# Attention's y in memory: from group by row by token, to token tile by row by group

## What is computed

```python
y = y + jnp.einsum('bhqk,bhkd->bhqd', ascores, av)
y = y.transpose(0, 2, 1, 3).reshape(B, T, C)
attn_out = jnp.einsum('btc,oc->bto', y, w_proj)
x = x + ga * attn_out
h = layernorm(x) * (1 + cb) + sb
logits = einsum('bsh,he->bse', h, gate_w)      # top 2 of 8, softmax of the two
x = x + gb * ffn(h)                            # ffn: the two chosen experts, weighted
```

## Time and profile before

| | us |
|---|---|
| median of 3 runs | 2641.78 (2641.4 to 2646.95) |
| the profiled execution's own time | 2640.58 |
| its span, first to last instruction | 2638.8 |
| attention, by the trace | about 780 to 1920 |
| projection of tiles 2 to 15 | 1928.9 to 2148 |
| expert loop | 2193 to 2626 |

### The profile page before, as it was taken

The page is one execution under the profiler, slowest core; times in us unless marked ns, Lnnn a source line. Parts: engine busy times, 40 slices in busy tenths (PEclk is TensorE's granted clock), DMA queues, the critical chain, the costliest instruction groups (busy, mean ns, idle before and its releaser), DMA issues. The chain is left out here.

```text
span 2638.8 us, 39402 instructions
## 1 busy us (share of the span) xinstructions
PE 2439.7 (92%) x13343; PEld 1605.5 (61%) x13343; DVE 1595.9 (60%) x3212; ACT 1061.0 (40%) x1896; POOL 1210.8 (46%) x825
## 2 busy tenths in 40 slices
PE   6789999899789999999999999998978978999997
PEld 4676777787654444444444444444467766888885
DVE  5544555501077777777777777777146564677765
ACT  3420111111155555555556565555512113444443
POOL 3451423300057767676767676667601122333332
PEclk9999999999889999999999999999989988999998
DMA  7346555421385233333324241513277846879875
GB/s 274 112 132 209 170 165 163 122 85 40 75 258 118 60 94 85 85 94 85 93 73 105 59 112 50 110 44 102 60 236 185 188 98 249 299 279 324 306 273 180
DMA packets 229523, 386.15 MB, mean 146 GB/s; under 512 B 44212, under 2 KB 100980, under 8 KB 229236
## 3 DMA queue, kind: packets, MB, share of 16 engines
q1 hardware_dynamic: 201652, 308.18, 41.1%
q0 software_dynamic: 17152, 50.38, 5.5%
q10 hardware_dynamic: 10560, 25.54, 3.3%
HBM read 285.00 MB, written 106.38 MB: 148 GB/s over the span
## 5 line engine op out<-in xcount | busy, mean ns | idle before, releaser
L1462 POOL TENSOR_TENSOR t_two<-t_prob 128x1024 f32<-128x1024 f32 (+1 forms) x320 | 688.4, 2171 | 172.6 <-ACT t_prob L1310 109.3
L1310 ACT ACTIVATE t_prob<-t_scores_psum 128x512 f32<-128x512 f32 (+3 forms) x1280 | 610.5, 537 | 376.3 <-PE t_scores_psum L1115 188.1
L1342 DVE TENSOR_REDUCE t_part<-t_seen_psum 128x1 f32<-128x512 f32 x768 | 480.8, 682 | 148.2 <-PE t_seen_psum L1093 143.6
L1093 PE MATMUL t_seen_psum<-t_k_stack,t_q_stack 96*128 96x512 f32 (+3 forms) x1283 | 512.7, 405 | 31.7 <-DVE t_part L1342 15.3
L1115 PE MATMUL t_scores_psum<-t_q_stack,t_k_stack 97*128 97x512 f32 (+3 forms) x1280 | 504.1, 405 | 6.3 <-ACT t_prob L1310 5.0
L1115 PEld LDWEIGHTS t_scores_psum<-t_q_stack,t_k_stack 97*128 97x128 f32 x1280 | 243.2, 191 | 304.1 <-ACT t_prob L1310 168.4
L1348 DVE CUSTOM_DVE_ANT_0 t_seen_psum<-t_seen_psum,t_causal 128x128 f32<-128x128 f32 (+3 forms) x515 | 250.5, 504 | 101.9 <-PE t_seen_psum L1093 90.9
L1137 PE MATMUL t_y_acc_psum<-t_prob,t_v 128*32 128x512 f32 (+3 forms) x2560 | 301.9, 544 | 0.0
L1093 PEld LDWEIGHTS t_seen_psum<-t_k_stack,t_q_stack 96*128 96x128 f32 x1283 | 252.2, 197 | 67.2 <-DVE t_part L1342 29.9
L1762 PE MATMUL acc_psum<-z_e_hi,z_x_hi 128*128 128x512 f32 x576 | 228.3, 396 | 0.0
L1764 PE MATMUL acc_psum<-z_e_hi,z_x_lo 128*128 128x512 f32 x576 | 225.4, 391 | 0.0
(11 more groups left out here) (247 smaller groups left out, 3733.1 us busy)
## 6 DMA issues: line engine op xcount, KB each, us to landing
z_raw<-in_expert_w SPq DMA_DIRECT2D x80, 512.0 KB, 6.2
z_spare<-in_expert_w SPq DMA_DIRECT2D x72, 512.0 KB, 6.9
f_w_raw<-in_wmod SPq DMA_DIRECT2D x8, 2048.0 KB, 9.8
t_q_stack<-scratch_q_hi SPq DMA_DIRECT2D x64, 256.0 KB, 5.0
t_k_stack<-scratch_k_hi SPq DMA_DIRECT2D x64, 256.0 KB, 5.3
f_w_raw<-in_w_attn SPq DMA_DIRECT2D x24, 512.0 KB, 6.6
t_both<-scratch_inverse SPq DMA_DIRECT2D x132, 64.0 KB, 2.1
t_y<-scratch_a_y SPq DMA_DIRECT2D x33, 256.0 KB
```

What stands on the lines that cost most here:

```text
L1093: nc.tensor.matmul(seen[:, n % BANKS, 0:width], q_stack[par][0:STACK, h, t0:t0 + P], k_stack[par][0:STACK, h, c * CH:c * CH + width], star ...
L1310: nc.scalar.activation(prob[:, step % RING, h, c0:CH], scores[:, score_bank(step, h), c0:CH], ACT.Exp, scale=1.0 / math.sqrt(D)).then_inc( ...
L1342: nc.vector.tensor_reduce(dst, seen[:, n % BANKS], AX.X, ALU.max).then_inc(seen_free, 1)
L1462: nc.gpsimd.tensor_tensor(two[:, pair % 2, heads, c0:CH], a, b, ALU.add).then_inc(two_ready, 1)
```

## The change

The two tensors of y lie in memory as [NT, P, G, P]: token tile, row of the group (partition), group, token of the tile. A store of one unit then writes, for each of the 4 token tiles of its quarter, 128 tokens of each partition: pieces of 512 bytes, 512 pieces instead of 128. A load of one token tile reads 4 KB in one piece for each partition, 128 pieces instead of 1024. The amounts are the same, and so are the instructions of all engines and their order; in SP's stream only the shapes of the 66 stores and 32 loads of y differ (128x512 becomes 128x4x128, 128x8x128 becomes 128x1024).

```diff
@@ attention: store(i, wi)
-                    sp.dma_start(dst[group_of(i, wi), :, qc * CH:(qc + 1) * CH].rearrange("g p n -> (g p) n"),
-                                 src).then_inc(stored, 16)
+                    sp.dma_start(dst[qc * TPC:(qc + 1) * TPC, :, group_of(i, wi), :].rearrange("t p g n -> p t (g n)"),
+                                 src.rearrange("p (t n) -> p t n", n=P)).then_inc(stored, 16)
@@ attention: loads of the first two token tiles
-                                sp.dma_start(dst.bitcast(F32), src[:, :, n * P:(n + 1) * P].rearrange("g p n -> p g n")).then_inc(tokens_loaded[n], 16)
+                                sp.dma_start(dst.bitcast(F32), src[n]).then_inc(tokens_loaded[n], 16)
@@ tail: load_y(n)
-                    sp.dma_start(dst[:, n % 2].bitcast(F32), src[:, :, n * P:(n + 1) * P].rearrange("g p n -> p g n")).then_inc(y_loaded[n % 2], 16)
+                    sp.dma_start(dst[:, n % 2].bitcast(F32), src[n]).then_inc(y_loaded[n % 2], 16)
@@ adaln_block
-    y_hi, y_lo = scratch("y_hi", [G, P, T]), scratch("y_lo", [G, P, T])
+    y_hi, y_lo = scratch("y_hi", [NT, P, G, P]), scratch("y_lo", [NT, P, G, P])
```

## The result

The change makes the kernel slower. Its median is 2653.78 us (20 runs, 2640.48 to 2668.82) against 2645.02 for the kernel before (20 runs, 2633.91 to 2662.73): ratio 1.0035, interval 1.0021 to 1.0049, about 9 us. The forecast of 2628 was wrong in size and sign. The profiled execution took 2656.89 us.

The account below looks back on a forecast made before the run. PE, busy 92% of the span, bounds the kernel, so only its waits and low clock can be won. Gains of 3.2 + 4.3 + 4.6 + 0.8 = 12.9 us from 2640.58 give 2627.7, forecast 2628, range 2618 to 2641.

Parts of the forecast that it names:

- Stores ... I cost them at nothing: Attention: stores of y go from 2 KB to 512-byte pieces, costed at nothing, with SP's 8.2 us to spare.
- Term A: Start of the tail: cheaper y loads let DVE's constants land sooner, gain 3.2 us, bounds 1.6 to 5.2.
- Terms B and C: Tail beside scatters: y lands sooner; tiles 8 and 9 gain 4.3 us, tiles 12 and 13 gain 4.6.
- the factor on y's time: Tail loads beside a scatter: 4 KB packets take 0.78 (510 ns) of eight small ones' 656; between 0.50 and 0.88.
- the scatter sets the pace: Tail beside a scatter: piece size does not matter, only 3.2 us at the tail's start is gained, 2637.4; chance 0.20.
- a packet sticks: Tail: 4 KB load packets stick beside a scatter, deciding from about 740 ns; kernel slower, 2650 us; chance 0.12.
- The clock term: Tail, tiles 9 and 13: shortened waits lose less clock, gain 0.8 us for both, between 0 and 3.
- the stores are dear after all: Stores of y: 512-byte pieces take 5 us instead of 2, mattering only together with something unseen; chance 0.02.

Follow-up runs that it names:

- old_small_stores: Kernel before, old order of y, each run of 128 tokens padded to 160, so stores and loads are in 512-byte pieces: 2650.05 us, 1.0040.
- late scatters: Kernel before and changed kernel, each with all scatters held back until the projection's tiles are turned: 2654.82 us (1.0050) and 2666.47 us (1.0096).
- before_early: Kernel before (also called early), with SP issuing the store of y ahead of the broadcasts of the next unit's inverse: 2626.61 us, 0.9950.
- best: Kernel before, with the store ahead of the inverse's broadcasts and the reload between the inverse's store and those broadcasts: 2622.06 us, 0.9932.
- paced: Kernel before, with the scatters of the first three batches spread, one pair behind each turned tile: 2643.64 us, 1.0019.
- after_best: Changed kernel, with the store ahead of the inverse's broadcasts and the reload between the inverse's store and those broadcasts: 2624.39 us, 0.9946.
- new_padded: Changed kernel with a ninth, unused group, so that rows of y lie 4.5 KB apart instead of 4 KB: 2645.19 us, 1.0015.
- after_early: Changed kernel, with SP issuing the store of y ahead of the broadcasts of the next unit's inverse: 2628.63 us, 0.9947.
- old_large_loads: Kernel before, old layout and 2 KB stores, y loaded in 4 KB pieces in wrong order, comparable only up to the experts: 2706.44 us, 1.0223.
- new_small_loads: Changed kernel, same layout and small stores, loads of y cut into 512-byte pieces by taking even and odd groups apart: 2657.72 us, 1.0066.

## Why the prediction was wrong

**The step that failed first: "Stores ... I cost them at nothing".** Its cover was "nobody in attention waits for them but the reload of the adapter's part steps later", with SP's 8.2 us to spare. That slack is the end of the stage. The reload itself had none: DVE already waited 12.7 us for it in 15 places, and the row was there to be read. I named the waiter and did not ask whether it was late. In its place the runs showed that the small stores cost about 9 us: old_small_stores pays 1.0040 with nothing changed but the pieces and their padding. And three edits that take this chain off the path (no reload, store first, reload first as well) bring the medians of the two layouts to -5.6, +2.0 and +2.3 us of each other, where they are 8.8 and, with late scatters, 11.7 us apart. One such pair alone says little. With 95% intervals that I estimate from the single runs, the means differ by 9.8 +- 4.4 us (before and after), 4.6 +- 5.8 (their repeats) and 11.9 +- 3.2 (late scatters), and without the chain by -4.8 +- 6.2, 0.3 +- 5.7 and 2.4 +- 4.8. The three without it average -0.7 +- 3.1. So the cost goes away with the chain. What in the chain the small stores make longer is another question.

**How a small piece makes the chain longer is shown only in part.** The landing of one store was the wrong measure: over the eight units of an execution whose reload follows a store within about 5 us (the short units, one for each group, as in the case above), from the issue of `y_hi`'s store to the reload's issue takes 4.15 us on the mean before and 3.84 after, so a small store is not late itself, as the earlier trace rows had said. What stands behind it in the queue is late. The load of v issued right behind the stores landed so, before and after, in the window around the case above:

```profile
t_v<-scratch_v SPq DMA_DIRECT2D x1, 256.0 KB, 3.1
```
```profile
t_v<-scratch_v SPq DMA_DIRECT2D x1, 256.0 KB, 4.0
```

Over all 28 loads of v in 780:1925 the median is 3.6 us before and 3.7 in its repeat, and 4.0 and 3.9 in the two profiles of the kernel after. From the reload's issue to DVE's sum it is, over the short units, 3.9 to 4.3 us in five kernels with 2 KB stores in the original order, and 4.3 to 4.7 in seven with small ones. But the two effects nearly cancel: from the store's issue to the sum it is 8.17 us on the mean of the five and 8.30 on that of the seven, 0.13 us longer, while DVE's wait there is 0.26 us longer (1.12 and 1.38 per unit). DVE's wait for the reload is 11.3 to 14.1 us in the one kind and 14.1 to 18.5 in the other. That is 3 us more on the mean, of which PE's idle time shows 1.9; most of the rest of the 6 us of the table is clock, by the estimate above. Why waits that are so little longer cost so much clock stays open, and whether the packets of the store themselves hold the queue or the many rows of memory that they touch was not told apart.

**Term A, 3.2 us forecast.** DVE's constants did come sooner: its wait for them fell from 5.17 us to 3.23, by 1.9 us and not by 3.2,

```profile
1950.10 1.28 DVE L1884 SCALAR_TENSOR_TENSOR z_h<-z_x,z_mv,z_scale 128x1024 f32<-128x1024 f32 x1 [3.23 <-DMA z_gate_w<-in_gate_w]
```

the wait before tile 0's transpose fell from 2.33 to 0.67 us, and tile 4 starts 37.1 to 38.5 us behind tile 2 in five kernels of the new layout against 39.0 to 39.4 with the old order in memory. With tile 2's own wait shorter by 0.7, A measured is about 2, in the forecast's bounds but not its 3.2. The mechanism held. Undisturbed, the packets of 4 KB were cheaper than eight of 512 bytes, but not as cheap as the 148 ns that I took; 1978:1985 answers to the earlier trace rows:

```profile
q1 hardware_dynamic: 413, 1.52, 62.7%
q10 hardware_dynamic: 9, 0.04, 1.3%
```

70 us for 413 packets are 170 ns each, against 252 for eight of 512 bytes before. But 42 of the 413 are under 512 bytes; if these cost nothing, the 371 of 4 KB took 189 ns. With 189 for 148 the prediction's own sum gives 1.0 us per tile and A = 2.0, which is what came. By the Trainium skill ("DMA: Bandwidth & Descriptors", "Why small descriptors are slow (HBM only)") it would have been 14% less; measured it is 33% less by the one count and 25% by the other, and the measurement decides.

**Terms B and C, 8.9 us forecast, about 0 measured.** The failing number is "the factor on y's time ... I take 0.78". Beside the first scatter, in 2020:2034:

```profile
q1 hardware_dynamic: 366, 1.37, 96.7%
q0 software_dynamic: 102, 0.00, 0.6%
```

96.7% of 16 engines for 14 us over 366 packets are 592 ns each, 0.90 of the 656 of eight small ones; and in 2083:2098, beside the second,

```profile
q1 hardware_dynamic: 182, 0.68, 59.9%
```

it is 790 ns, 1.20. By 4 KB moved, as I had counted rows 10 and 11, it is 648 and 866 ns, 0.99 and 1.32. So a packet of 4 KB costs there what eight of 512 bytes do, or more. Tile 8 came in time, since A and the shorter queue gave it a start; `y_lo` of tile 9 landed after 22.5 us where it took 21.9, and that of tile 13 after 21.2:

```profile
z_y_lo<-scratch_y_lo SPq DMA_DIRECT2D x1, 512.0 KB, 22.5
```
```profile
z_y_lo<-scratch_y_lo SPq DMA_DIRECT2D x1, 512.0 KB, 21.2
```

What the wait at tile 8 gave, the wait at tile 9 took. In the profiled executions tile 13 starts 174.7 to 178.4 us behind tile 2 in six kernels of the old order in memory (before, its repeat, early, best, paced, no reload), and 173.6 to 179.1 in five of the new: no difference. The rival "the scatter sets the pace" was right on the tail (I gave it 0.20); "a packet sticks" was right on the 790 ns but not on its price. All waits of PE for y in the tail, after, against 20.4 before (the number behind the last bar is idle time):

```profile
L1713 PE MATMUL acc_psum<-p_hi,z_y_hi 128*128 128x512 f32 x224 | 94.2, 420 | 22.7 <-DMA z_y_lo<-scratch_y_lo 22.7
```

**The clock term, 0.8 us forecast as a gain.** It was right that a wait can cost more than its length, but I looked for it in the tail alone. It also works in attention, where the waits are of 1 to 3 us and the clock cost 12 to 21 us in the profiles of these two kernels.

**The rival "the stores are dear after all"** held the answer, with a chance of 0.02 and "together with something that I do not see". What I did not see was a row of the profile before.

**Open.** In the front, which touches no y, the last matmul of L681 starts 527.7 to 531.1 us into the span in six of seven kernels of the unpadded new layout and at 522.1 to 526.5 in all thirteen others. From 500 to 505 us the granted clock was 0.50 after and 0.62 in its repeat, and 1.00 before, in after_best and in new_padded. after_best is the exception (522.1), and after_early, at 529.4, is as fast as before_early in the timed runs. No run tells what this is, and no run tested it. If it is real, it is some of the 9 us. Against its being much of it speaks old_small_stores, whose front is short (524.6) and which pays as much, and that the difference went with the chain; but each of those pairs is only known to about 5 us.

## What to carry to other kernels

Before a transfer is costed at nothing, look up every wait on whatever is released by it, and in whose queue it stands: an average wait of 0.8 us in the row of its waiter means that the cover is already used up, and slack at the end of a stage says nothing of the middle. Where PE is at 92%, price such a wait with the low-clock stretch that may follow it. Take no difference of one stage from two single profiles: the same kernel's attention differed by 9.9 us. Also look for what an in-order queue holds back: a store ready at 812 us that leaves at 817 was worth more (15 us, and 19 with the reload moved too) than the layout that was meant to help.

## What the hardware showed that I had not expected

- Waits of PE of 1 to 3 us can be followed by a low clock, and not in proportion to their length: over the next 12 us it was 0.57 after 2.69 us and 0.86 after 1.10, but 0.72 after 1.30 and 1.00 after 1.81. Without the wait it stayed at 1.00 over 20 us. The clock alone made 8 us between two profiles of one kernel's attention.
- Beside the scatters 4 KB packets took 592 and 790 ns, eight of 512 bytes 656. The size of the packet hardly matters there, but the distance of the rows may. In the 30 us from the start of the first scatter 2.75 to 3.47 MB moved in seven kernels whose loads read rows 4 KB apart (old_large_loads is one of them, and the 2.75 is new_small_loads, with pieces of 512 bytes), 3.29 to 3.60 in three with rows 4.5 KB apart, and 3.68 to 4.19 in six with the old order and small loads. And with rows 4.5 KB apart tile 13 started 169.3 to 172.9 us behind tile 2 in three of four kernels (176.8 with spread scatters), with 4 KB apart 173.6 to 179.1 in five. The timed runs do not separate the two once the stores are off the path (0.9932 against 0.9946, overlapping), so this is a hint.
- Loads that stand behind small stores in one queue land later though the stores themselves are not seen to: 4.0 and 3.9 us against 3.6 and 3.7 for 256 KB, medians of 28, in two profiles of each kernel.
